# Expert layer of a hybrid block kernel: chunk 0's second stage interleaved with chunk 1, shares of both loaded together

## What is computed

```python
scores = jax.nn.sigmoid(xt.astype(jnp.float32) @ gate_w.T)     # xt: 2048 x 128, 16 experts
biased = scores + gate_b
_, idx = lax.top_k(biased, TOPK)                               # 4 of 16
w = jnp.take_along_axis(scores, idx, axis=-1)
w = w / jnp.sum(w, axis=-1, keepdims=True)
w = w * ROUTE_SCALE
comb = comb.at[jnp.arange(T)[:, None], idx].add(w)             # 2048 x 16, mostly zeros
def expert_body(y, args):
    w13_e, w2_e, c_e = args
    h = _silu_and_mul(xt @ w13_e.T)                            # 64 wide
    return (y + c_e[:, None] * (h @ w2_e.T), None)
y, _ = lax.scan(expert_body, jnp.zeros_like(xt), (w13, w2, comb.T))
y = y + _silu_and_mul(xt @ w13_s.T) @ w2_s.T                   # one shared expert
```

## Time and profile before

| | us |
|---|---|
| median of 3 runs | 1088.47 |
| the runs | 1081.61, 1088.47, 1089.74 |
| the profiled execution, its own time | 1088.91 |
| its span (first to last instruction) | 1085.6 |
| busy: PE, DVE, ACT, POOL | 986.0, 568.1, 557.1, 147.7 |
| mean granted TensorE clock | 0.936 |

### The profile page before, as it was taken

How to read it: one execution, slowest core, us unless ns; L and a number is a source line. 1 busy time by engine, 2 the same in 40 slices (tenths; PEclk the granted TensorE clock), 3 DMA queues, 4 the chain that set the end, 5 groups by cost and what they waited for, 6 DMA issues and landing times.

```text
span 1085.6 us, 22121 instructions
## 1 busy us (share of the span) xinstructions
PE 986.0 (91%) x9464; PEld 455.1 (42%) x9464; DVE 568.1 (52%) x1126; ACT 557.1 (51%) x767; POOL 147.7 (14%) x164
## 2 busy tenths in 40 slices
PE   7578998989999998997989798997999999999898
PEld 3345665343333334685333243443433333344343
DVE  4465763473333437566555544555666666524454
ACT  5113445468999985643555562227454554455121
POOL 3300101023100101211001031000123223004000
PEclk9569999999999999757999899999999999998999
DMA  9653311001000000000000007510000000001841
GB/s 298 162 141 88 84 31 43 0 1 41 2 2 2 2 2 0 3 4 4 1 0 1 0 2 144 133 36 1 1 2 2 2 2 2 1 1 26 160 112 56
DMA packets 18809, 43.27 MB, mean 40 GB/s; under 512 B 5324, under 2 KB 5772, under 8 KB 17164
## 3 DMA queue, kind: packets, MB, share of 16 engines
q1 hardware_dynamic: 18712, 41.87, 15.9%
HBM read 37.07 MB, written 4.55 MB: 38 GB/s over the span
## 4 chain that ended last, share of the span: by engine, by line
PE 74%; DVE 9%; ACT 8%; DMA 4%; issue 3%; SPq 1%; POOL 0%; DVEq 0%; POOLq 0%
PE ps L1584 73%; DMA stf<-scr_w 1%; ACT nrr L799 1%; ACT nrr L797 1%; DMA stf<-aux 1%; SPq L518 1%; DVE mxq L1202 1%; DVE masked L1196 1%; ACT work L1047 1%; DMA stf<-scr_k 1%; DVE work L1156 1%; DVE work L1538 1%; ACT work L1041 0%; DMA x<-in_x 0%; ACT nrr L786 0%
## 5 line engine op out<-in xcount | busy, mean ns | idle before, releaser
L1584 PE MATMUL ps<-rq,stf 32*64 32x512 f32 (+4 forms) x4096 | 209.9, 466 | 3.0 <-ACT hz L950 1.6
L1584 PE MATMUL ps<-work,vbuf 64*32 64x96 f32 (+8 forms) x3200 | 201.6, 404 | 2.4 <-issue 1.3
L1584 PE MATMUL ps<-hz,wsb 128*128 128x512 f32 (+1 forms) x352 | 161.1, 618 | 4.0 <-ACT nsq L788 3.5
L906 ACT ACTIVATE work<-ps 128x1024 f32<-128x1024 f32 x144 | 139.4, 1022 | 13.4 <-PE ps L1584 10.2
L1584 PEld LDWEIGHTS ps<-rq,stf 32*64 32x64 f32 x4096 | 99.3, 150 | 107.0 <-issue 85.0
L1584 PEld LDWEIGHTS ps<-work,vbuf 128*32 128x32 f32 (+1 forms) x3200 | 72.7, 120 | 117.3 <-issue 65.1
L968 ACT ACTIVATE work<-ps 128x1024 f32<-128x1024 f32 x72 | 73.6, 1023 | 75.7 <-PE ps L1584 75.7
L845 ACT ACTIVATE work<-ps 128x768 f32<-128x768 f32 x64 | 51.6, 811 | 99.8 <-PE ps L1584 99.7
L1584 PE MATMUL ps<-work,wsb 128*128 128x512 f32 (+1 forms) x176 | 90.6, 610 | 10.4 <-DVE work L1473 7.7
L1584 PEld LDWEIGHTS ps<-hz,wsb 128*128 128x128 f32 (+1 forms) x352 | 62.2, 190 | 83.4 <-issue 68.2
L1016 ACT ACTIVATE work<-ps 128x512 f32<-128x512 f32 x48 | 28.7, 597 | 124.4 <-PE ps L1584 124.4
(11 more groups left out here) (195 smaller groups left out, 1247.1 us busy)
## 6 DMA issues: line engine op xcount, KB each, us to landing
stf<-scr_w SPq DMA_DIRECT2D x128, 128.0 KB, 4.0
wsb<-in_w SPq DMA_DIRECT2D x1, 3440.0 KB, 21.5
stf<-scr_k SPq DMA_DIRECT2D x12, 204.0 KB
stf<-scr_q SPq DMA_DIRECT2D x12, 192.0 KB
csb<-in_c SPq DMA_DIRECT2D x1, 2099.0 KB, 9.2
rq<-in_rq SPq DMA_DIRECT2D x2, 1024.0 KB, 5.1
scr_q<-work SPq DMA_DIRECT2D x6, 256.0 KB, 7.0
scr_k<-work SPq DMA_DIRECT2D x6, 256.0 KB, 6.2
```

The lines of the kernel that those rows point to most:

```text
L906: nc.scalar.activation(probs_of(n)[:, 2 * k:2 * k + 2].rearrange("p h s -> p (h s)"), two(slot(2 * n + k)), ACT.Exp, scale=SCALE).then_inc ...
L1584: return nc.tensor.matmul(o, l, r, start=start, stop=stop, skip_group_check=True)
```

## The change

The second stage no longer goes chunk by chunk. `PAIRS` lists (0,0), (1,0), (0,1), (1,1) and so on to (1,7), then chunks 2 and 3 as before. Gate and up of chunk 1's next pair stand ahead of chunk 1's down. The rows of chunks 0 and 1 are transposed together behind a = 5, those of chunks 2 and 3 behind a = 6 and 7. One store takes the rows of both chunks, and each expert's row is loaded for both at once, 256 KB, into two neighbouring rooms. Products and sums stay what they were.

```diff
--- before.py
+++ after.py
@@ -427,9 +427,24 @@
                 return moe[:, 5, a]
             return early[:, a - 2] if a < 8 else later[:, a - 8]
 
+        PAIRS = [(c, j) for j in range(NPAIR) for c in (0, 1)] + [(c, j) for c in (2, 3) for j in range(NPAIR)]
+        ITEMS = len(PAIRS)
+
+        def late_downs(i, n):
+
+            last = [c for c, j in PAIRS[:n + 1] if j == NPAIR - 1]
+            return (ITEMS - NC) * i + n + 1 - len(last)
+
+        def share_of(i, n):
+
+            c, j = PAIRS[n]
+            room = n % SHARES - (c if c < 2 else 0)
+            uses = [m for m in range(ITEMS) if m % SHARES == room and PAIRS[m][0] != 1]
+            return room, len(uses) * i + uses.index(n - (c if c < 2 else 0)) + 1
+
         AHEAD = 2 + NPAIR
         ROUTE_STEPS = 12
-        ROUTED = 5
+        ROUTE_AT = {5: (0, 1), 6: (2,), 7: (3,)}
 
 
         SETS = [
@@ -506,29 +521,31 @@
             x_load(3)
             def shares(i):
 
-                def store(c):
-                    sp.wait_ge(m_cs, NC * i + c + 1)
-                    sp.dma_start(scr_w[:, c * CH:(c + 1) * CH], cwt[:, c * CH:(c + 1) * CH]).then_inc(m_st[c], 16)
-
-                def load(c, j):
-                    k = (i * NC + c) * NPAIR + j
+                def store(c, n):
+                    sp.wait_ge(m_cs, NC * i + c + n)
+                    sp.dma_start(scr_w[:, c * CH:(c + n) * CH], cwt[:, c * CH:(c + n) * CH]).then_inc(m_st[c], 16)
+
+                def load(n, wide):
+                    c, j = PAIRS[n]
+                    k = ITEMS * i + n
+                    room, _ = share_of(i, n)
                     if k >= SHARES:
-                        sp.wait_ge(m_h, k - SHARES + 1)
+                        sp.wait_ge(m_h, k + wide - SHARES)
                     for e in range(2):
-                        sp.dma_start(share[HB * e:HB * (e + 1), k % SHARES],
-                                     scr_w[2 * j + e, c * CH:(c + 1) * CH].unsqueeze(0).broadcast_to([HB, CH]))\
-                            .then_inc(m_w[k % SHARES], 16)
-
-                store(0)
+                        sp.dma_start(share[HB * e:HB * (e + 1), room:room + wide].rearrange("p k s -> p (k s)"),
+                                     scr_w[2 * j + e, c * CH:(c + wide) * CH].unsqueeze(0).broadcast_to([HB, wide * CH]))\
+                            .then_inc(m_w[room], 16)
+
+                store(0, 2)
                 sp.wait_ge(m_st[0], 16 * (i + 1))
                 for j in range(NPAIR):
-                    load(0, j)
-                for c in range(1, NC):
-                    store(c)
-                for c in range(1, NC):
+                    load(2 * j, 2)
+                for c in (2, 3):
+                    store(c, 1)
+                for c in (2, 3):
                     sp.wait_ge(m_st[c], 16 * (i + 1))
                     for j in range(NPAIR):
-                        load(c, j)
+                        load(NPAIR * c + j, 1)
 
             sp.wait_ge(s_zero, 1)
             zeros = aux[0:B * NG * 3 * D // 2, 0:G * PAD].bitcast(BF16)
@@ -1005,15 +1022,13 @@
                         act.wait_ge(e_m, k - 1)
                     nc.scalar.activation(moe[:, 3, a % 2], bank(a % 2), ACT.Silu)
                     nc.scalar.activation(moe[:, 4, a % 2], bank(2 + a % 2), ACT.Copy).then_inc(e_a, 1)
-                    if ROUTED < a <= ROUTED + NC:
-                        rows(a - ROUTED - 1)
-                for c in range(1, NC):
-                    for j in range(NPAIR):
-                        k = (i * NC + c) * NPAIR + j
-                        act.wait_ge(m_gu, full(i, c, j) + 1)
-                        if full(i, c, j) >= 2:
-                            act.wait_ge(m_su, full(i, c, j) - 1)
-                        nc.scalar.activation(moe[:, 0, k % 2], bank(k % 2), ACT.Silu).then_inc(m_sg, 1)
+                    for c in ROUTE_AT.get(a - 1, ()):
+                        rows(c)
+                for f in range(full(i, 1, 0), full(i, 1, 0) + ITEMS - NPAIR):
+                    act.wait_ge(m_gu, f + 1)
+                    if f >= 2:
+                        act.wait_ge(m_su, f - 1)
+                    nc.scalar.activation(moe[:, 0, f % 2], bank(f % 2), ACT.Silu).then_inc(m_sg, 1)
 
 
             LOG_EXP = "natural_log_exp_and_others"
@@ -1458,30 +1473,30 @@
                                                     in1=tot.unsqueeze(2).broadcast_to([P, nt, NE]),
                                                     op0=ALU.mult, op1=ALU.mult))
                 assert step[0] == k0 + ROUTE_STEPS
-                for c in range(NC):
-                    for j in range(NPAIR):
-                        k = (i * NC + c) * NPAIR + j
-                        if k >= 2:
-
-                            if j != 1:
-                                dve.wait_ge(m_y, ((k - 2) // NPAIR) * (NPAIR - 1) + (k - 2) % NPAIR + 1)
-                            else:
-                                dve.wait_ge(s_lin, outputs((U_M0, U_M1)[i], c - 1))
-                        if c == 0:
-                            dve.wait_ge(e_m, AHEAD * i + 3 + j)
-                            dve.wait_ge(m_w[k % SHARES], 32 * (k // SHARES + 1))
-                            nc.vector.tensor_tensor(moe[:, 2, k % 2], hidden_of(2 + j), share[:, k % SHARES],
-                                                    ALU.mult).then_inc(m_h, 1)
-                            continue
-                        dve.wait_ge(m_sg, full(i, c, j) + 1)
-                        nc.vector.tensor_tensor(moe[:, 1, k % 2], bank(2 + k % 2), moe[:, 0, k % 2], ALU.mult)\
-                            .then_inc(m_su, 1)
-                        dve.wait_ge(m_su, full(i, c, j) + 1)
-                        dve.wait_ge(m_w[k % SHARES], 32 * (k // SHARES + 1))
-                        nc.vector.tensor_tensor(moe[:, 2, k % 2], moe[:, 1, k % 2], share[:, k % SHARES],
-                                                ALU.mult).then_inc(m_h, 1)
-                        if j == 1:
-                            residual(U_M0 if i == 0 else U_M1, x, c - 1)
+                u = (U_M0, U_M1)[i]
+                for n, (c, j) in enumerate(PAIRS):
+                    k = ITEMS * i + n
+                    room, loads = share_of(i, n)
+                    if n >= 2:
+                        if PAIRS[n - 2][1] < NPAIR - 1:
+                            dve.wait_ge(m_y, late_downs(i, n - 2))
+                        else:
+                            dve.wait_ge(s_lin, outputs(u, PAIRS[n - 2][0]))
+                    elif k >= 2:
+                        dve.wait_ge(s_lin, outputs(U_M0, NC - 1))
+                    if c == 0:
+                        dve.wait_ge(e_m, AHEAD * i + 3 + j)
+                        product = hidden_of(2 + j)
+                    else:
+                        f = full(i, c, j)
+                        product = moe[:, 1, f % 2]
+                        dve.wait_ge(m_sg, f + 1)
+                        nc.vector.tensor_tensor(product, bank(2 + f % 2), moe[:, 0, f % 2], ALU.mult).then_inc(m_su, 1)
+                        dve.wait_ge(m_su, f + 1)
+                    dve.wait_ge(m_w[room], 32 * loads)
+                    nc.vector.tensor_tensor(moe[:, 2, k % 2], product, share[:, n % SHARES], ALU.mult).then_inc(m_h, 1)
+                    if n in (17, 19, 25):
+                        residual(u, x, (n - 17) // 2 if n < 25 else 2)
                 residual(U_M0 if i == 0 else U_M1, x, NC - 1)
 
             norm(0)
@@ -1956,13 +1971,13 @@
                     mm(bank(4 + c), wd[rows], moe[rows, 5, c // 2], True, False)
 
                 def gate_up(c, j):
-                    k, f = (i * NC + c) * NPAIR + j, full(i, c, j)
+                    f = full(i, c, j)
                     if c == 1 and j < 2:
                         pe.wait_ge(e_a, AHEAD * (i + 1))
                     else:
                         pe.wait_ge(m_su, f - 1)
-                    mm(bank(k % 2), w_("w_gate")[:, j * P:(j + 1) * P], ch(z, c))
-                    mm(bank(2 + k % 2), w_("w_up")[:, j * P:(j + 1) * P], ch(z, c)).then_inc(m_gu, 1)
+                    mm(bank(f % 2), w_("w_gate")[:, j * P:(j + 1) * P], ch(z, c))
+                    mm(bank(2 + f % 2), w_("w_up")[:, j * P:(j + 1) * P], ch(z, c)).then_inc(m_gu, 1)
 
                 def route_rows(c):
                     pe.wait_ge(m_d, ROUTE_STEPS * (i + 1))
@@ -1971,8 +1986,9 @@
                                                   rt[:, (4 * c + tt) * NE:(4 * c + tt + 1) * NE], c_("ident"))
                     ins.then_inc(m_t, 1)
 
-                def down(c, j):
-                    k = (i * NC + c) * NPAIR + j
+                def down(n):
+                    c, j = PAIRS[n]
+                    k = ITEMS * i + n
                     pe.wait_ge(m_h, k + 1)
                     return mm(bank(4 + c), w_("w_down")[:, j * P:(j + 1) * P], moe[:, 2, k % 2], False, j == NPAIR - 1)
 
@@ -1980,17 +1996,16 @@
                     pe.wait_ge(s_ws, 16)
```

(15 more changed lines are left out.)

## The result

The changed kernel took 1079.09 us (median of 12 runs, 1075.70 to 1083.35), the kernel before on the same chip 1087.22 (12 runs, 1081.61 to 1092.13): a ratio of 0.9918, 95% interval 0.9900 to 0.9936. The forecast was 1080.3, with 1073.5 to 1087 as its range. It set out from 1088.47, the median of three runs; from the 1087.22 of twelve the same 8.2 us lead to 1079.0.

The account below looks back on a forecast made before the run. TensorE was taken as the bound, an edit being worth the idle time it removes; savings of 3.9 us (layer 1) and 4.3 (layer 0), together 8.2, led from the 1088.47 median to 1080.3, range 1073.5 to 1087.

Parts of the forecast that it names:

- The bound: Chunk 0's second stage: TensorE's downs wait for VectorE, and VectorE for the shares; 12.5 us hold 7.3 us of work.
- The start of the stage: Second stage: gate and up of chunk 1's first pair start 0.1 us behind ScalarE's last early copy.
- The first landing: First wide share: lands 1004.8 to 1005.0, product done 1005.5 to 1005.8, 0.2 to 0.5 us before its down.
- my 0.04: Joined store of chunks 0 and 1: doubling its bytes was put at 0.04 us.
- The step: Interleaved pairs: one gate and up plus two downs take 3.43 us; VectorE's three operations are in time, nothing charged.
- The sum: Layers from gate and up (1,0) to the end: 75.5 us; saved 3.9 in layer 1, 4.3 in layer 0, together 8.2.
- the cover of the transfers: Interleaved stage: 512 KB a step takes 3.05 to 3.54 us; even at 148 GB/s share 7 is covered by 0.7 us.
- the signs to look for: New profile: no TensorE idle until the last down, downs two by two every 3.43 us, wide pairs 3.0 to 3.6 apart.
- Rivals B and C: Transfers bound the interleaved stage: B, 135 GB/s, 1084.1 us, chance 0.09; C, 107 GB/s, slower than before, chance 0.03.
- Rival D: First product misses its down: landing 2 us later loses 1.5 to 1.8 us per layer, 1083.6; chance 0.07.
- Rival A: TensorE's clock: one fall more or less gives 1083.5 or 1077 us; chance 0.16 lower, 0.07 higher.

Follow-up runs that it names:

- the narrow loads: Changed kernel's order of pairs, rows and store, but each expert's row loaded for one chunk at a time (128 KB); ratio 0.9923 to the kernel before.
- the two layouts: Kernel before, own order, routing-weight rows in memory 10 KB apart, or chunk by chunk 2 KB apart, instead of 8 KB; ratios 0.9930 and 0.9951.
- the run with more traffic: Changed kernel with 384 KB of needless transfers behind each of the eight wide pairs of loads; layers 76.62 and 78.69 us, one run.
- the one with 128 partitions: Kernel before, own order, both rows of a pair loaded by one 256 KB transfer to all 128 partitions; 1267.42 us.

## Why the prediction was right

**The bound.** That chunk 0's second stage waits for the shares and that the interleaved order fills the wait held: TensorE's waits there, 3.7 us in layer 1 and 4.1 in layer 0 by the profile, are gone, and the narrow loads show that the order does it without the wide loads. Rows and store joined are in both of these kernels; alone they cost 1.1 us a layer.

**The start of the stage.** Gate and up (1,0) were put 0.1 behind the copy; they came 0.05 behind.

**The first landing.** I had 5.3 to 5.6 us from the first wide issue to the product; it was 997.90 - 992.88 = 5.0. The issue itself came 0.3 later against the copy than I said, since the wider store took 1.91 us to the first load instead of 1.58, so my 0.04 for it was too low. The two errors nearly cancel, and 0.6 us were in hand where 0.2 to 0.5 were forecast.

**The step.** 3.43 us and nothing charged for VectorE's three operations: as measured, with 1.42 idle.

**The sum.** 75.5 us from gate and up (1,0) to the last down; measured 75.56 in layer 1 and 75.80 in layer 0, which was 0.35 longer than layer 1 before as well. The sum took layer 1's work for both layers, and so put layer 0's saving 0.3 too high. Savings 3.9 and 4.3 forecast, 3.91 and 4.02 found. That the medians differ by 8.1 where 8.2 were forecast is closer than they can tell: their interval stands for 7.0 to 10.9 us. The layers' lengths, 7.9, are the better witness.

**What was off: the cover of the transfers.** "Even the slow rate is covered, by 0.7 us" was right in sign, but the term was mis-sized. A step of 512 KB takes 2.3 us at 229 to 231 GB/s, not 3.05 to 3.54, and the wide pairs landed that close until the rooms held them back, not 3.0 to 3.6 us apart as the signs to look for had it. I read 148 GB/s as what the DMA engines can do, because they were busy 0.97. They were busy with loads of 2 KB pieces from rows 8 KB apart, as the two layouts show. Rivals B and C, priced on 135 and 107 GB/s, were therefore much farther off than their 0.12. I also let a bound for 64 partitions at a time speak for this (SBUF — State Buffer, Door 1, in the Trainium skill). The 229 to 231 GB/s of the changed kernel and the 243 to 278 in the run with more traffic are above what half of the ports would give by that page, 8 x 27.2 = 218. Loads to the two halves follow each other and may overlap; no run separates this.

**Rival D** did not come, and its price holds about where it was set. In the run with more traffic the first product came 1.8 and 1.3 us later against the last early copy, and TensorE waited 0.96 and 0.82 us, at the full clock. What it left out is what a longer delay does: with a wait of 3 us the lower clock comes on top. **Rival A** was real as noise, and nothing shows it as an effect of the change: the clock differs between executions ahead of layer 0, and the stretch between the layers took 268.2 us in both profiles, but 267.0 to 270.8 over the profiles of the table (the one with 128 partitions left aside).

## What to carry to other kernels

Where a stage waits for transfers, put the independent work of the next stage into its gaps, and check the one moment at which the first transfer is needed; waits of 3.0 and 3.3 us there cost 4.7 and 6.3. A DMA queue that is busy 0.97 need not be at its limit: try another pitch of the rows in memory before the order of a program is rebuilt, since here one constant gave about 3 of the 4 us. Where runs scatter by 0.5%, measure the edited stage between two instructions that the edit doesn't touch.

## What was not expected of the hardware

- Loads of 128 KB, broadcast in 2 KB pieces and each from a row 8 KB behind the last: 148 GB/s with the DMA engines busy 0.97. From rows 10 KB or 2 KB apart: 200 GB/s and more, at SP's issue rate, busy 0.55 to 0.76. The Trainium skill (DMA: Bandwidth & Descriptors, Latency and other measured facts) reports the like for pitches of 2 MB and more, there between the partitions of one copy; here it was 8 KB between one load and the next. Loads of 256 KB, in 4 KB pieces, ran at 225 to 231 GB/s with either pitch, 8 or 10 KB. That it lies in the memory's channels is not shown.
- 3.3 us without a matmul, behind a sparse stretch, and TensorE ran at 0.50 for about 6 us; 3.0 us, and it did for 3.4. Waits of 0.2 to 1.2 us in the same stage left it at 1.00.
- A transfer to 128 partitions whose source has 2 rows ran on few engines: 54 GB/s, with the DMA engines busy 0.15.
